# A two-layer transformer kernel: score features in (dimension, head) order, 12 stack transfers a turn, GpSimd work in halves, and a new order of the pieces

## The reference

```python
xn = layernorm(x)                                  # both layers
q, k, v = xn @ Wq.T, xn @ Wk.T, xn @ Wv.T          # q and k are rotated by position
pattern = softmax(causal(q @ k.T * 32 ** -0.5))    # per head
attn = (pattern @ v) @ Wo.T
mlp0 = (silu(xn @ w_gate.T) * (xn @ w_up.T)) @ w_down.T              # layer 0, 2048 hidden
mlp1 = (silu((xn @ gate_w.T) * gate_s) * ((xn @ up_w.T) * up_s)) \
       @ down_w.T * down_s                                           # layer 1, 1408 hidden
x = x + attn + mlp
```

## Time and profile before

| what | value |
|---|---|
| three runs | 2048.77, 2055.16 (median), 2058.95 us |
| profiled execution | 2055.59 us, span 2053.8 us |
| TensorE busy | 1866.4 us, 91% of the span |
| VectorE, ScalarE, GpSimd busy | 54%, 52%, 34% |
| mean granted TensorE clock | 0.958 of full speed |
| bytes moved | 126.20 MB, 61 GB/s |

### The profile page before, as it was taken

The page is one execution under the profiler, slowest core; times in us unless marked ns, Lnnn a source line. Parts: engine busy times, 40 slices in busy tenths (PEclk is TensorE's granted clock), DMA queues, the critical chain, the costliest instruction groups (busy, mean ns, idle before and its releaser), DMA issues.

```text
span 2053.8 us, 25605 instructions
## 1 busy us (share of the span) xinstructions
PE 1866.4 (91%) x8656; PEld 1347.6 (66%) x8656; DVE 1116.6 (54%) x2432; ACT 1060.1 (52%) x2353; POOL 703.4 (34%) x516
## 2 busy tenths in 40 slices
PE   4999999999899899898889999999988998998987
PEld 3777767775675666656467777776757756575654
DVE  6554647373755564736346465573746636455452
ACT  2464646556256473646425646464652555646363
POOL 3225243242341533333213243534314415233320
PEclk9999999999999899999779999999999999999989
DMA  4213113031130313103213131311401403121201
GB/s 159 67 42 98 42 44 90 27 99 41 52 88 22 87 47 73 42 21 109 72 62 78 37 92 42 84 56 29 122 11 52 101 9 98 42 68 37 66 7 41
DMA packets 59874, 126.20 MB, mean 61 GB/s; under 512 B 9440, under 2 KB 10464, under 8 KB 58720
## 3 DMA queue, kind: packets, MB, share of 16 engines
q1 hardware_dynamic: 59744, 124.57, 22.0%
HBM read 69.48 MB, written 4.19 MB: 36 GB/s over the span
## 4 chain that ended last, share of the span: by engine, by line
PE 69%; DVE 11%; ACT 6%; SPq 5%; issue 5%; POOL 3%; DMA 2%; DVEq 0%; ACTq 0%; POOLq 0%
PE D L905 15%; PE G L905 11%; PE U L905 8%; PE OE L999 7%; PE SS L983 6%; PE OE L905 6%; PE SS L905 6%; SPq L564 5%; PE OE L983 3%; PE OE L962 3%; PE SS L962 2%; DVE OE L826 2%; ACT OE L618 2%; ACT pr L634 2%; DMA QS<-pr 1%
## 5 line engine op out<-in xcount | busy, mean ns | idle before, releaser
L874 DVE TENSOR_TENSOR xres<-D,xres 128x512 f32<-128x512 f32 x352 | 243.1, 691 | 214.1 <-PE D L905 209.7
L634 ACT ACTIVATE pr<-SS 128x512 f32<-128x512 f32 (+3 forms) x512 | 232.2, 501 | 143.8 <-PE SS L983 135.5
L709 POOL TENSOR_TENSOR hl<-tt,hh 128x512 fp32r<-128x512 f32 x108 | 139.0, 1287 | 475.7 <-ACT hh L651 475.7
L618 ACT ACTIVATE OE<-OE,mp 128x384 f32<-128x384 f32 (+3 forms) x256 | 203.4, 795 | 104.9 <-DVE mp L826 104.0
L826 DVE CUSTOM_DVE_ANT_0 OE<-OE,mask 128x384 f32<-128x384 f32 (+3 forms) x256 | 220.5, 873 | 50.6 <-PE OE L962 49.7
L618 ACT ACTIVATE SS<-SS,mp 128x128 f32<-128x128 f32 (+3 forms) x256 | 162.2, 634 | 95.7 <-DVE mp L826 94.0
L728 POOL TENSOR_SCALAR_AFFINE_SELECT pr<-pr 128x512 f32<-128x512 f32 x128 | 81.0, 635 | 378.7 <-ACT pr L634 378.7
L826 DVE CUSTOM_DVE_ANT_0 SS<-SS,mask 128x128 f32<-128x128 f32 (+3 forms) x256 | 167.6, 673 | 64.3 <-PE SS L962 63.0
L905 PE MATMUL G<-xh,wgh 128*128 128x512 f32 x432 | 178.0, 412 | 24.0 <-DVE tt L885 22.8
L983 PE MATMUL SS<-QS,KS 98*128 98x512 f32 (+2 forms) x512 | 182.1, 413 | 14.9 <-ACT pr L634 12.3
L905 PE MATMUL D<-wdh,hh 128*128 128x512 f32 x432 | 174.2, 403 | 19.6 <-DVE xres L874 13.7
(11 more groups left out here) (123 smaller groups left out, 3733.6 us busy)
## 6 DMA issues: line engine op xcount, KB each, us to landing
KS<-pr SPq DMA_DIRECT2D x192, 128.0 KB, 2.3
QS<-pr SPq DMA_DIRECT2D x192, 128.0 KB, 2.3
raw<-in_wgate_dram SPq DMA_DIRECT2D x27, 512.0 KB, 3.7
raw<-in_wup_dram SPq DMA_DIRECT2D x27, 512.0 KB, 3.7
raw<-in_wdown_dram SPq DMA_DIRECT2D x27, 512.0 KB, 3.7
raw<-in_wqk_dram SPq DMA_DIRECT2D x16, 512.0 KB, 4.4
val<-in_x_dram SPq DMA_DIRECT2D x4, 1024.0 KB, 6.9
trig<-in_wv_dram SPq DMA_DIRECT2D x4, 1024.0 KB, 5.6
```

The lines of the kernel that those rows point to most:

```text
L618: act.activation(s, s, ACT.Exp, bias=mp[:, c, at:at + 1], scale=-1.0, accum_out=se[:, c, at:at + 1]) \
L634: act.activation(weights(i)[:, h, skip:W], SB[(i * HG + h) % 3][:, skip:W], ACT.Exp, scale=-1.0) \
L709: pool.tensor_tensor(hl[:, fc, :], tt[:, (blk * nfc + fc) % 2, :], hh[:, fc, :].bitcast(F32), ALU.subtract) \
L874: dve.tensor_tensor(xres[:, rt, :], d[:, :], xres[:, rt, :], ALU.add).then_inc(sem["v_dfree"], 1)
```

## The change

- The features of four heads lie in (dimension, head) order in the projection's output, so that one dimension's four heads are neighbours. The weights' high and low parts are written in that order (`heads_apart`), the rotation's swap partner is 4 partitions away and not 1, and the cos and sin table is loaded in four transfers to match. One stack transfer then carries all four heads: 12 a turn of 256 KB, where there were 24 of 128 KB.
- The projections run K, Q of columns 0 and then K, Q of columns 1, and each rotation is followed by its own three transfers. The first 16 score tiles wait for the first six (`d_stack`), the others for all (`d_later`).
- GpSimd subtracts 512 columns at a time, also in the value weights' split.
- The value weights' split comes later at the start and at the borders. In the opening all values come ahead of the last two projections.
- `keep` is a transfer from memory in place of ScalarE's copy. `guess` is done on ScalarE alone. Some waits are dropped where an earlier one covers them.
- Gate and up products are cut in three pieces, and `PACE` has new strings.

```diff
-GU_PARTS = 2
+DIGITS = "0123456789abcdefghijklmnopqrstuvwxyzABCDEFGHIJKLMNOPQRSTUVWXYZ"
+GU_PARTS = 3
...
     if l == 0:
         rows = [piece + [("row", 1, rt)] for rt, piece in enumerate(d0)]
         rows[-1] += normal(1)
-        pieces += rows + g1[GU_PARTS:] + output(1) + [piece + [("row", 1, TPC + i)] for i, piece in enumerate(d1)]
+        pieces += rows + g1[3:] + output(1) + [piece + [("row", 1, TPC + i)] for i, piece in enumerate(d1)]
         items += norms(1, range(TPC))
+        items[-3].append(("v_weights", 1))
     else:
         d0[-1].append(("store", 0))
         d1[-1].append(("store", 1))
-        pieces += d0 + g1[GU_PARTS:3 * GU_PARTS]
+        pieces += d0 + g1[3:9]
         if not final:
-            items[-1] += [("x_next",), ("v_weights", 0)]
+            items[-1] += [("x_next",)]
             items += [[("row", 0, rt) for rt in range(TPC)] + normal(0)] + norms(0, range(TPC))
+            items[-3].append(("v_weights", 0))
             pieces[-1].append(("keep", 0))
-        pieces += output(1) + g1[3 * GU_PARTS:] + d1
+        pieces += output(1) + g1[9:] + d1
...
-    return [("stats", layer, 0)] + [("v_weights", 1)] * layer + [("xn", layer, 0), ("xn", layer, 1)]
+    return [("stats", layer, 0), ("xn", layer, 0), ("xn", layer, 1)]
...
-    out += [values[4], ("rotate", 0), proj[1], values[5], ("rotate", 1), proj[2], values[6], ("rotate", 2), proj[3], values[7],
+    out += [values[4], ("rotate", 0), proj[1], values[5], values[6], values[7], ("rotate", 1), proj[2], ("rotate", 2), proj[3],
-START = [("row", 0, rt) for rt in range(TPC)] + [("stats", 0, 0), ("v_weights", 0), ("xn", 0, 0), ("xn", 0, 1)]
-START += [x for piece in norms(0, range(TPC)) for x in piece] + [("keep", 0)]
+START = [("row", 0, rt) for rt in range(TPC)] + normal(0)
+START += [x for piece in norms(0, range(TPC)) for x in piece] + [("v_weights", 0), ("keep", 0)]
...
-         "007000101010011001120212010211111110200100200000000000000000000000000000000000000000000000006021"),
+         "00400020100120011013020311130203111010111002000000110010000101110000000010010000010010000012w021"),
-        ("00500010111110010023030311111111110000000000000000000000000000000000000000000000000000000000000000000",
+        ("01300021010101020113031110111121111030010010010000110010001100100001000000000000000000000000000000000",
...
+    def fresh(self, rt):
+
+        return self.b not in self.written.get(rt, {})
+
+    def close(self, rt):
+
+        return self.written.get(rt, {}).get(self.b, 0) > self.n["v_dfree"] - 1
...
+        def heads_apart(kind, t):
+
+            return t.rearrange("p (g k h) -> p g h k", h=HG, k=DH) if kind == "A" else t
...
                 sp.wait_ge(sem["g_wv"], n("g_wv", 1))
-                sp.dma_start(trig[:, :, :], rope[layer]).then_inc(sem["d_rope"], 16)
-
-            def rows(dram, n, c):
-                return dram[n.b, c * W:(c + 1) * W, :].rearrange("(t p) d -> p t d", p=P)
+                for h in range(HG):
+                    sp.dma_start(trig[h:P:HG, :, :], rope[layer, h * DH:(h + 1) * DH]).then_inc(sem["d_rope"], 16)
+
+            def rows(dram, n, c, b):
+                return dram[b, c * W:(c + 1) * W, :].rearrange("(t p) d -> p t d", p=P)
+
+            def keep(n, c):
+                sp.wait_ge(sem["d_out"], n("d_out"))
+                sp.dma_start(xres[:, c * TPC:(c + 1) * TPC, :], rows(x, n, c, n.batches)).then_inc(sem[f"d_keep{c}"], 16)
...
-                if t % NC < NC - 1:
-                    return
-                qk = t // NC
+                qk, c = t % 2, t // 2
+                cols = slice(c * W, (c + 1) * W)
                 flats = ((flat_h, flat_h, flat_l), (flat_h, flat_l, flat_h))[qk]
                 sp.wait_ge(sem["g_rl"], n("g_rl", 1))
                 if qk:
                     sp.wait_ge(sem["p_v"], n("p_v"))
-                for h in range(HG):
-                    for r, src in enumerate(flats):
-                        at = slice(r * DH, (r + 1) * DH)
-                        sp.dma_start((QS[at, :, h, :] if qk else KS[at, h, :]).bitcast(F32),
-                                     src[qk][h * DH:(h + 1) * DH, :]).then_inc(sem[f"d_stack{h}"], 16)
+                for r, src in enumerate(flats):
+                    at = slice(r * DH, (r + 1) * DH)
+                    sp.dma_start((QS[at, c, :, :] if qk else KS[at, :, cols]).bitcast(F32), src[qk][:, cols]) \
+                        .then_inc(sem["d_later" if c else "d_stack"], 16)
...
-            def keep(n, c):
-                act.wait_ge(sem[f"d_x{c}"], n(f"d_x{c}", 16))
-                act.wait_ge(sem["d_out"], n("d_out"))
-                act.copy(xres[:, c * TPC:(c + 1) * TPC, :], val[:, c * TPC:(c + 1) * TPC, :]) \
-                    .then_inc(sem["a_keep"], 1)
...
             def guess(n, c):
-                act.wait_ge(sem["v_lse"], n("v_lse", 2))
+                act.wait_ge(sem["a_nat"], n("a_nat"))
+                act.activation(y0[:, :], se[:, c, :].bitcast(I32), ACT.Copy, scale=LN2 / 2 ** 23, bias=-(127 - 0.043) * LN2).then_inc(sem["a_log"], 1)
+                act.wait_ge(sem["a_log"], n("a_log", 1))
                 act.activation(ex[:, :], y0[:, :], ACT.Exp, scale=-1.0).then_inc(sem["a_log"], 1)
...
-                act.wait_ge(sem["p_pv"], n.at("p_pv", i - RING + 1))
+                if h == 0:
+                    act.wait_ge(sem["p_pv"], n.at("p_pv", i - RING + 1))
...
-                return pool.tensor_tensor(flat(lo), src[:, 0:SIZE[kind]], flat(hi).bitcast(F32), ALU.subtract)
+                for at in range(0, SIZE[kind], W):
+                    part = slice(at, at + W)
+                    ins = pool.tensor_tensor(heads_apart(kind, flat(lo)[:, part]), heads_whole(kind, src[:, part]),
+                                             heads_apart(kind, flat(hi)[:, part]).bitcast(F32), ALU.subtract)
+                return ins
...
-                pool.tensor_tensor(wvl, wv_raw, wvh.bitcast(F32), ALU.subtract).then_inc(sem["g_wv"], 1)
+                for c in range(KC):
+                    ins = pool.tensor_tensor(wvl[:, c, :], wv_raw[:, c, :], wvh[:, c, :].bitcast(F32), ALU.subtract)
+                ins.then_inc(sem["g_wv"], 1)
...
-                dve.stream_shuffle(swapped[:, t % 2, :], src[:, :], [i ^ 1 for i in range(32)]).then_inc(sem["v_swap"], 1)
+                dve.stream_shuffle(swapped[:, t % 2, :], src[:, :], [i ^ HG for i in range(32)]).then_inc(sem["v_swap"], 1)
...
-                dve.wait_ge(sem["v_dfree"], n("v_dfree"))
+                if n.fresh(rt):
+                    dve.wait_ge(sem[f"d_keep{rt // TPC}"], n(f"d_keep{rt // TPC}"))
+                if n.close(rt):
+                    dve.wait_ge(sem["v_dfree"], n("v_dfree"))
...
-                qk = 1 - t // NC
+                cols = slice(t // 2 * W, (t // 2 + 1) * W)
+                qk = 1 - t % 2
...
-                if c == 0 and qb == 0:
-                    pe.wait_ge(sem[f"d_stack{h}"], n(f"d_stack{h}"))
-                if t < 4:
+                if t == 0:
+                    pe.wait_ge(sem["d_stack"], n("d_stack"))
                     pe.wait_ge(sem["v_al"], n("v_al"))
                     pe.wait_ge(sem["a_val"], n("a_val"))
+                if t < 4:
+                    held = 1 if n.turns == 0 else 3
+                    pe.wait_ge(sem["v_swap"], n("v_swap", min(0, t - held)))
                 elif c == 0:
                     pe.wait_ge(sem["a_nat"], n("a_nat", -3))
                 elif t == HG * TPC:
+                    pe.wait_ge(sem["d_later"], n("d_later"))
```

More of the change, by code:

```diff
@@ L199, in plan @@
         g1, d1 = ([[x for x in p if x[0] != "w"] for p in q] for q in (g1, d1))
[L200 removed]
+    pieces += g0[:3] + late + g0[3:] + g1[:3]
     if l == 0:
@@ L367, in did @@
             self.b, self.layer = step[1:]
+        if step[0] == "keep":
+            self.n[f"d_keep{step[1]}"] += 16
+        if step[0] == "x_next":
+            self.batches += 1
+        if step[0] in ("add_wo", "add_down"):
+            rt = step[1] * TPC + step[2]
+            self.written.setdefault(rt, {})[self.b] = self.n["v_dfree"] + 1
         if step[0] == "turn":
@@ L372, in did @@
             self.n[sem] += k
-        if step[0] == "proj" and step[1] % NC == NC - 1:
-            for h in range(HG):
-                self.n[f"d_stack{h}"] += STACKS
+        if step[0] == "rotate" and step[1] < 2:
+            self.n["d_stack"] += STACKS
+        elif step[0] == "rotate":
+            self.n["d_later"] += STACKS
         if step[0] == "w":
@@ L889, in gated @@
                     .then_inc(sem["v_h"], 1)
-            walk(dict(v_weights=v_weights, row=row, stats=stats, xn=xn_, norm=norm, proj=proj, rotate=rotate, nat=nat, guess=guess, better=better, log=log_, flip=flip, heads=heads_, add_wo=add_wo, add_down=add_down, gated=gated))
```

(1 more changed line is left out.)

85 lines of the change are left out of this document (39 added, 46 removed).

## The result

The changed kernel takes 2064.39 us, the median of 10 runs (2062.01 to 2066.68), against 2053.72 us for the kernel before beside it (10 runs, 2045.9 to 2061.08). The ratio is 1.0053, 95% interval 1.0039 to 1.0068. It is slower, by 0.5%. I had forecast 1982 us, and gave slower a chance of 7%.

The account below looks back on a forecast made before the run. TensorE, busy 91% of the span, was taken as the bound, with its idle and slow-clock time in question. Layer 0 -5, layer 1 -58.8, start -3.5, batch border -6: together -73.3, from 2055.6 to 1982 us; range 1925 to 2035.

Parts of the forecast that it names:

- Projections and stacks: Term for projections and stack transfers: last three transfers land 10 us after projection 2; layer 0 -16.5, layer 1 -18.0 us.
- proj: A turn's stretch of 4 projections, rotations, stack transfers and pieces before the next nat; forecast 21 us, bounds 19 and 26.5.
- a wait of 0.5 to 2 us: TensorE's remaining wait per turn for the last stack transfers before the first nat tiles.
- nat: A turn's stretch of 32 score tiles; forecast 43 to 45 us each, layer 0 -8.8, layer 1 -17.8 us.
- values: Stretch from a layer's first value product to its first nat; forecast 3.2 us of pieces fewer per layer.
- C: Rival: spread stacks at 70 GB/s make each of 12 proj stretches wait 7.4 us longer; 2078 us, chance 0.05.
- My sentence on ports: Stack transfers reaching 32 partitions use 8 of 16 ports, about 218 GB/s at best, so halving their count gains nothing.
- st: A turn's stretch of 48 exponentials with value products between; forecast layer 0 -7, layer 1 +9.6 us, apart from turn 3's block.
- Rival A: Tile alternation holds nat at 46 us whatever surrounds it; 2014 us, chance 0.20.
- The block in turn 3: Layer 0's last st up to the border's first transpose, taking moved pieces; 50.75 to 84 us, +33, bounds 76 and 95.
- Batch border: Between batches, ScalarE no longer waits for the store; -6 us, bounds 0 and -12.
- a sign of being wrong: Layer 0 longer by over 10 us, listed among signs that would show the forecast wrong.

Follow-up runs that it names:

- e1: Changed kernel with each stack transfer reading the first 32 adjacent partitions four times over instead of all 128 once; 2009.6 us, ratio 0.9766 to the kernel before.
- e7: Changed kernel with each stack transfer split into two 128 KB halves, each reading 64 adjacent partitions and written with a step of 2; 2011.95 us, ratio 0.9779.
- e9: e7 with the query and key weights laid out in (dimension, head) order before the launch; 1994.45 us, ratio 0.9698 to the kernel before.
- e8: Changed kernel with the query and key weights laid out in (dimension, head) order before the launch; 2058.88 us, ratio 1.0004 to the kernel before.
- e15: e9 with GpSimd's weight subtractions whole again, the value weights' too; 1995.55 us, ratio 0.9732 to the kernel before.

## Why the prediction was wrong

**The step that failed** is the landing in the term "Projections and stacks": "three transfers at 2 x 0.63 each = 3.8, and about 2.3 to land the last", with "Bytes per turn are equal" as its reason. Two things in it were wrong.

1. The rate. 207 GB/s was carried over, and the changed kernel's stretch ran at 124. The 0.63 us of the kernel before were SyncE's pace of issuing, which is the same for 256 KB (three in 1.9 us), and not a rate. 256 KB in 2 x 0.63 us was possible: e1's land one every 1.3 us. With the changed kernel's partitions they land one every 2.05 us.
2. What stands in front. The sum counts the three Q transfers alone. In the turn shown the first Q transfer is issued at 176.11, the last of the three K ones lands at 180.39, and the last Q one at 186.59. From that first issue it is 10.5 us, where the sum has 3.8 + 2.3 - 0.6 = 5.5.

So the 21 us of proj became 25.7, and "a wait of 0.5 to 2 us" became one of 5.46. Nearly all of the waiting is there: 63 of the 65.0 us that matmuls wait for stacks stand at the first tiles of the 16 nats, 2 at later ones. The run that gives the rate back (e7) takes 52.4 us off the medians (56 by the ratios); it brings proj to 21.0, 21.35 and 22.17, and values to 3.2 us each under the kernel before, as forecast. Its nat is 10 us longer in all than the changed kernel's, where the order of the weights (below) comes in: with that cured on both sides, nat takes 728.0 us in all with the changed kernel's transfers (e8) and 714.0 with e7's (e9). So most of the slow rate's cost lay in proj, and some in nat.

The reading of the earlier trace rows was wrong as well, though the sum doesn't use it: TensorE's matmuls waited 19.3 us for stacks and not 46.2, and 15.3 of these at two of the 16 nats, one of which the earlier trace rows shows. The forecast for proj rested more on moving matmuls out of it than on waits won.

**The rivals.** C was the right mechanism, at chance 0.05. I priced it at 70 GB/s for no row, and said it decides only from a rate under 80. The threshold was off: 124 GB/s sufficed, because I left out the three K transfers that the Q ones queue behind, and what stands in a layer's opening. "No such pattern is in the trace" should have raised the chance of C and widened the range, not lowered it: it ended at 2035, 29 us short. The output weights queued behind the transfers land after 13.7 us; what that costs no run shows. My sentence on ports, "the trace agrees", took 32 partitions on the written side to settle the rate; the 207 of the trace was the pace of the issues, so it bore out no limit, and e1 and the changed kernel write the same 32 and differ by 197 to 124.

**A term that was missing.** I costed nothing for writing the rounded query and key weights in another order. It doubles ScalarE's instruction (2.04 for 1.04 us, 16 times) and adds 0.27 to each of GpSimd's 32 halves. With e7's transfers it is worth 17.5 us (e7 to e9): nat is 21.7 us shorter in all, while proj and st together are 7.7 longer. With the changed kernel's transfers it is worth 5.5 to 10 (after to e8).

**What is left.** Medians: 2064.4 - 52.4 (rate) - 17.5 (order of the weights) = 1994.5, which is 12.5 above 1982. Nat is 18 us over (714.0 for 695.7) and proj 8 (260.3 for 12 x 21), while st is 7 under (767.3 for 703.7 + 71). Rival A, a floor at 46 in layer 0, holds in part: e9 has 45.56, 46.41, 45.10 and 43.24 for my 44, 43.5, 43.5 and 45. What sets this floor no run has taken apart.

**What held and what didn't.** St of layer 0: 40.63, 41.18, 42.83 (forecast 41.5, 41, 42.5). St of layer 1: 41.73, 39.49, 39.27 (39.5, 40, 39.5), two of the three longer, as said. The block in turn 3: 80.70 (84). Batch border 29.89 to 24.23 (-6). No layer border's normalization over 0.55 us. Layer 0 was to be shifted at equal length, and layer 1 to be 29 us shorter. In the changed kernel the first batch's layer 0, from its first projection, takes 510.2 us for 491.7, so it is longer by over 10 us, a sign of being wrong that the prediction names; layer 1 takes 497.0 for 500.9. In e9 they take 493.2 and 476.6, and there the two statements hold within some 5 us. That GpSimd's halves would be worth nothing beyond start and borders held in e15; there the moved step did the work, not the halves.

## What to carry to other kernels

In these runs a copy between partitions had a rate of its own for each pattern of partitions read and written, and equal bytes didn't settle it. A time of one transfer that equals the time of its issue tells the issuer's pace and not the rate. And what is queued ahead of a transfer belongs in its landing. So where a change makes a pattern that the trace doesn't show, the rate is to be bounded from half of the known one (99 against 199 here), and checked first by an experiment that leaves the program as it is and changes only the source's partitions. When one slow resource is cured, price the edits that lay in its shadow again; the same edit was worth 5 to 10 us before and 17 after. And an access that changes its step is an edit with a cost, even where the count of elements stays.
